# Layer norm of x in a Mamba scan kernel: two steps on VectorE, the power on GpSimd, taken earlier

## The chip, the cores and the metric

The kernel runs on one core of a Trainium2 chip. The metric is the device time of one execution in microseconds (us). Engines are named as the profile names them: PE is TensorE's matmul (PEld its weight load), DVE is VectorE, ACT is ScalarE, POOL is GpSimd, SP is SyncE, which issues the loads and stores here.

## The reference

One transformer-like block over x of 2 x 4096 x 256 in fp32. Only the first line bears on the change:

```python
h = _layernorm(x, axis=-1) * (1 + ca) + sa        # (x - m) / sqrt(v + 1e-5) over the 256 features
x = x + ga * _L0_attn_ref(h, ...)                 # two Mamba scans (backward and forward), sigmoid, mean, norm
h = _layernorm(x, axis=-1) * (1 + cb) + sb
x = x + gb * _L0_ffn_ref(h, ...)                  # 256 -> 1024 gated -> 1024 -> 1024 -> 256
```

Each Mamba scan projects h to 512 inner channels, convolves over time, and runs the recurrence `h = a * h + bx` for 16 states of each channel.

## The kernel before

Time is cut into chunks of 512 steps. There are 8 chunks for each of two batches, so 16 in a pass. Pass one (`ps == 0`) runs the backward scan, and pass two the forward scan. After both, a second stage does the join and the feed-forward layers, also in 16 chunks.

In a pass, the work of one chunk is written out by hand as 32 units (`NU`), numbered k = 0 to 31. A unit is one of 16 states for one half of the channels. It has two scan tiles of 128 x 512, one after the other on DVE (steps 2k and 2k+1). Every engine has its own loop over the units and runs it in order; semaphores tie the loops together:

- POOL, at unit k: `weigh_b(k)` makes the product dBx that the scan of unit k adds (for 27 of 32 units, `B_UNITS`; the other five, 19, 22, 25, 28 and 31, take it from PE). Then `weigh_c(k - 4)` scales the scanned state of 12 of the units (`P_UNITS`: 1, 2, 5, 9, 13, 15, ...). Then, at some units, small steps for the next chunks.
- ACT, at step g = 2k or 2k+1: `decay(g)` makes the exponentials that scan tile g needs, at most three tiles ahead of DVE (it waits until tile g - 3 is scanned). Behind it come the evacuations of the next chunk's matmuls.
- DVE, at unit k: the two scans (`scan`), which wait for the product (`dbx`) and for the decays (`da`); gates of some units; `weigh_c(k - 4)` for the other 20 units; at last the norm's step of this unit.
- PE does the projections, the convolution and the transposes of the states.

The norm of x runs two chunks ahead, only in pass one: in 14 of its chunks, for the chunk two further on. The first two chunks' norms are done in the prologue. The steps, all counted on the one semaphore `ln`, are:

1. DVE at unit 4: four `bn_stats` (L1435). At unit 5: four `bn_aggr` (L1441), which leave the mean in `mv[:, :, 0]` and the variance in `mv[:, :, 1]`. DVE does these at the end of the unit, behind its scans.
2. POOL at unit 8 (`RSTD_S`), behind `weigh_b(8)` and `weigh_c(4)` (unit 4 is not one of POOL's, so only `weigh_b(8)` stands there): four operations on 128 x 4 values, L1317 adds epsilon, L1319 raises to the power -1/2, L1321 multiplies by the mean, L1323 multiplies by -1.
3. ACT at step 18 (`AT_XN`), that is unit 9, behind `decay(18)` and other work of that step: `norm_x` waits for `ln` to reach 6 and writes the normalised x in four activations (L1165). The next item in ACT's order is `decay(19)`.
4. SP stores it (`store_xn`), and PE transposes it one chunk later (`front`).

Of the kernel before, what the change touches and what calls it, by code (L numbers as in the profile page):

```python
# [9 lines left out]
ALU = mybir.AluOpType  # L10
# [2 lines left out]
P = 128  # L13
BATCH, SEQ, DM = 2, 4096, 256
DI, DS, DCONV, DTR, DH = 512, 16, 4, 64, 1024
LNK = 7
T = 512
NC = SEQ // T
NCH = BATCH * NC
# [9 lines left out]
EPS = 1e-5  # L29
# [44 lines left out]
AT_XN = 18  # L74
AT_EXP = (51, 57)
AT_LNP = (51, 57)
NORM_STAT, NORM_AGGR, RSTD_S = 4, 5, 8
AT_XD = (15, 19, 20, 21)
ADD_S = (29, 0)
U_S = (30, 11)  # L80
# [284 lines left out]
def mamba(nc, a, bank, ident, cols, mod, gain, norm_c, fcol, any_odd, passes, w1, w2, J, x_v, yb_v, yf_v, xn_v, b_dram,  # L365
# [11 lines left out]
    with ExitStack() as c:  # L377
        def sb(name, shape):
            return c.enter_context(nc.sbuf_tensor(f"m_{name}", shape, F32))
# [7 lines left out]
        mv = sb("mv", [P, TS, 6])  # L387
# [161 lines left out]
        def _(sp):  # L549
# [8 lines left out]
            def load_x(ch):  # L558
                if rev(ch):
                    wait(sp, S["ln"], ch.at(LNK, 0))  # L560
                    sp.dma_start(xy[:, :, :], x_v[ch.batch, ch.time(True)]).then_inc(S["x_in"], 16)
# [8 lines left out]

            def store_xn(ch):

                sp.wait_ge(S["ln"], ch.at(LNK, 7))
                sp.dma_start(xn_v[ch.batch, ch.time(True)], xn[:, :, :]).then_inc(S["xn_out"], 16)

            def store_b(ch):
# [178 lines left out]
        def _(pe):  # L755
# [15 lines left out]
            def front(ch, g):  # L771
                q = ch.batch
                for k in range(KM):
                    if g == AT_LN[k]:

                        if k == 0:
                            if rev(ch):
                                pe.wait_ge(S["ln"], ch.at(LNK, 7))
                            else:
                                pe.wait_ge(S["xn_in"], ch.local(16, 16))  # L780
                        turn(J_LN[k], lambda s: xn[:, s, k * P:(k + 1) * P], ch)
                for m in range(KI):
                    k = g - AT_X[m]
                    if 0 <= k < KM:
                        if m == 0:
                            if ch.opens() and ch.batch == 0 and k == 0:
                                pe.wait_ge(S["w_in"], 48 * (ch.ps + 1))
                            wait_drained(pe, ch, J_LN[k])
                        part(ch, J_X[m], k, KM, w_in[:, k, m * P:(m + 1) * P], hT[:, k, :])
                    k = g - AT_CONV[m]  # L790
                    if 0 <= k < DCONV:

                        if k == 0:
                            if m == 0:
                                if ch.opens() and ch.batch == 0:
                                    pe.wait_ge(S["init"], SINIT + ch.ps)
                                pe.wait_ge(S["halo"], ch.at(2, 1))
                            if BANK[J_X[m]] != BANK[J_CONV[m]]:

                                wait_drained(pe, ch, J_X[m])  # L800
                        o = HALO - k if rev(ch) else k
                        part(ch, J_CONV[m], k, DCONV, diag[:, m * DCONV + k, :], xpre[:, m, o:o + T])
                    if g == (FIRST_DT if ch.first() else AT_DT)[m]:
                        if m == 0:
                            wait_drained(pe, ch, J_B)
                        part(ch, J_DT[m], 0, 1, w_dt[:, m * P:(m + 1) * P], dbB[0:DTR, :])
                    k = g - (FIRST_Z if ch.first() else AT_Z)[m]
                    if 0 <= k < KM:
                        part(ch, J_Z[m], k, KM, w_in[:, k, (KI + m) * P:(KI + m + 1) * P], hT[:, k, :])
                    if g == AT_B + m:  # L810

                        pe.wait_ge(S["xi"], ch.at(2, m // 2 + 1))
                        part(ch, J_B, m, KI, w_x[:, m, :], xi[:, m, :], B0 + 2 * DS)
                if g == (FIRST_C if ch.first() else AT_C):
                    rows = B0 + 2 * DS
                    wait_drained(pe, ch, J_B)
                    wait_free(pe, ch, J_C)
                    for t in range(TS):
                        mm = pe.transpose(FB[BANK[J_C]][:, t * rows:(t + 1) * rows], dbB[0:rows, t * P:(t + 1) * P],
                                          ident[0:rows, 0:rows])  # L820
                    mm.then_inc(fill[BANK[J_C]], 1)
# [188 lines left out]
        def _(act):  # L1010
# [145 lines left out]
            def norm_x(ch):  # L1156

                wait(act, S["xn_out"], ch.at(16, 0))
                if not ch.first():
                    act.sem_inc(S["go"], 1)  # L1160
                    wait_filled(act, ch.go(-1), J_LN[1])
                    act.sem_inc(S["go"], 1)
                act.wait_ge(S["ln"], ch.at(LNK, 6))
                for s in range(TS):
                    ins = act.activation(xn[:, s, :], xy[:, s, :], ACT.Identity, scale=mv[:, s, 3:4], bias=mv[:, s, 5:6])  # L1165
                ins.then_inc(S["ln"], 1)
# [146 lines left out]
        def _(pool):  # L1313
            def norm(ch):

                pool.wait_ge(S["ln"], ch.at(LNK, 2))
                pool.tensor_tensor(mv[:, :, 2], mv[:, :, 1], norm_c[:, 0, :], ALU.add).then_inc(S["ln"], 1)  # L1317
                pool.wait_ge(S["ln"], ch.at(LNK, 3))
                pool.tensor_tensor(mv[:, :, 3], mv[:, :, 2], norm_c[:, 1, :], ALU.pow).then_inc(S["ln"], 1)  # L1319
                pool.wait_ge(S["ln"], ch.at(LNK, 4))  # L1320
                pool.tensor_tensor(mv[:, :, 4], mv[:, :, 0], mv[:, :, 3], ALU.mult).then_inc(S["ln"], 1)  # L1321
                pool.wait_ge(S["ln"], ch.at(LNK, 5))
                pool.tensor_tensor(mv[:, :, 5], mv[:, :, 4], norm_c[:, 2, :], ALU.mult).then_inc(S["ln"], 1)  # L1323

            def add_dt(ch, half):
                q = ch.batch
# [102 lines left out]
        def _(dve):  # L1429
            def norm(ch, slot):  # L1430
                if slot == NORM_STAT:
                    dve.wait_ge(S["x_in"], ch.at(16, 16))
                    wait(dve, S["ln"], ch.at(LNK, 0))
                    for s in range(TS):
                        ins = dve.bn_stats(stat[:, s, :], xy[:, s, :])  # L1435
                    ins.then_inc(S["ln"], 1)
                if slot == NORM_AGGR:
                    dve.wait_ge(S["ln"], ch.at(LNK, 1))
                    dve.sem_inc(S["go"], 1)
                    for s in range(TS):  # L1440
                        ins = dve.bn_aggr(mv[:, s, 0:2], stat[:, s, :])  # L1441
                    ins.then_inc(S["ln"], 1)

            def gate(ch, g, m):
                q = ch.batch
                if g == AT_Y[m] + DVE_LAG:
                    dve.wait_ge(S["z"], ch.at(2, m // 2 + 1))
                    wait_filled(dve, ch, J_Y[m])
                    dve.tensor_tensor(z[:, q, m, :], FB[BANK[J_Y[m]]][:, :], z[:, q, m, :], ALU.mult
                                      ).then_inc(drain[BANK[J_Y[m]]], 1)  # L1450
# [31 lines left out]
            def body(ch):  # L1482
                for k in range(NU):
                    for m in range(2):
                        g = 2 * k + m
                        scan(ch, k, m)
                        if has(ch, -1):
                            for i in (2, 3):
                                gate(ch.go(-1), g, i)
                        for i in range(2):  # L1490
                            gate(ch, g, i)
                    old = unit(ch, k - W_LAG)
                    if old:
                        weigh_c(*old)
                    if norms(ch, 2):
                        norm(ch.go(2), k)

            def find_odd(n):

# [11 lines left out]
            def prologue(ch):  # L1511
# [2 lines left out]
                dve.memset(one_r[:, :], 1.0).then_inc(S["odd"], 1)  # L1514
                for s in range(NU):
                    norm(ch, s)
                dve.wait_ge(S["cols_in"], 32)
                for k in range(KI * DCONV):
                    ins = dve.tensor_scalar(diag[:, k, :], ident[:, :], cols[:, 0, COL_CW + k:COL_CW + k + 1], None, ALU.mult)
# [5 lines left out]
                for n in range(NPIECE):  # L1525
                    find_odd(n)
                    if n == 2:
                        for k in range(KM):
                            for b in range(BATCH):
                                last = dve.tensor_scalar(cbc[:, k, b, :], ident[:, :], 0.0, cs[:, k, b:b + 1], ALU.mult, ALU.add)  # L1530
                        last.then_inc(S["bcast_c"], 1)
                    if n == 3:
                        for s in range(NU):
                            norm(ch.go(1), s)
                dve.wait_ge(S["p_sum"], 2 * NPIECE)
                dve.tensor_reduce(odd_sum[:, :], YB[1][0:1, :], mybir.AxisListType.X, ALU.add).then_inc(S["odd"], 1)
                dve.wait_ge(S["odd"], 2)
# [371 lines left out]
```

## Time and profile before

| | |
|---|---|
| median of 3 runs | 4685.21 us (4684.75 to 4686.28) |
| the profiled execution | 4683.44 us |
| its span, first to last instruction | 4681.6 us |
| mean granted TensorE clock | 0.988 |
| PE, DVE, ACT, POOL busy, share of the span | 95%, 81%, 70%, 71% |

The two passes take the span up to about 3356 us, the feed-forward stage the rest. Shares of the whole span mix the two: POOL is almost unused in the second stage, PE almost never idle there. The stage that matters for the change is pass one, from about 76 to 1508 us, and there one chunk lasts 103.3 us.

### The profile page before, as it was taken

The page shows a single profiled execution, that of the slowest core. Times are in us where ns is not written, and L with a number is a line of the kernel's source. Part 1 is how long each engine was busy: PE and PEld are TensorE (multiplying, and loading weights), DVE is VectorE, ACT ScalarE, POOL GpSimd, SP SyncE. Part 2 cuts the span into 40 slices and gives each one's busy share as a digit, 9 for nine tenths or more (in the row PEclk, how much of TensorE's full clock was granted, in tenths as well). Part 3 has the DMA queues.
Part 4 walks back from the last instruction along what each step waited for, and adds up shares of the span by engine and source line. Part 5 has one row for each costly group of instructions (what it writes and reads, how often), then busy time and mean ns, then how long its engine had stood idle before and what let it go on. Part 6 is the DMA issues. An engine that isn't in the chain of part 4 may idle for free. (4 is left out here: it accounts for less than half of the span.)

```text
span 4681.6 us, 69073 instructions
## 1 busy us (share of the span) xinstructions
PE 4451.6 (95%) x24932; PEld 3375.9 (72%) x24932; DVE 3800.5 (81%) x4136; ACT 3279.4 (70%) x7067; POOL 3321.1 (71%) x1599
## 2 busy tenths in 40 slices
PE   8999999999999999999999999998899999999999
PEld 3676666667666666776666676666688888888888
DVE  6999999999999999999999999999754545444442
ACT  6788888888888877888888888888544444444443
POOL 5999999999999999999999999999710000000000
PEclk9999999999999999999999999999999999999999
DMA  8545444444554444444444445445411101010100
GB/s 296 175 136 150 146 142 138 141 136 140 148 146 138 147 138 140 136 143 143 138 139 132 135 137 147 142 134 158 164 62 35 34 23 37 32 37 32 37 23 10
DMA packets 297752, 545.90 MB, mean 117 GB/s; under 512 B 101888, under 2 KB 186624, under 8 KB 262784
## 3 DMA queue, kind: packets, MB, share of 16 engines
q1 hardware_dynamic: 296512, 529.91, 37.3%
q10 hardware_dynamic: 896, 11.54, 0.7%
q8 instruction: 199, 3.26, 0.3%
q14 instruction: 145, 1.19, 0.1%
HBM read 502.77 MB, written 50.14 MB: 118 GB/s over the span
## 5 line engine op out<-in xcount | busy, mean ns | idle before, releaser
L1472 DVE TENSOR_TENSOR_SCAN m_h<-bank,m_dBx 128x512 f32<-128x512 f32 x1728 | 2004.3, 1203 | 112.3 <-ACT bank L1205 82.4
L904 PEld LDWEIGHTS bank<-ident,m_h 128*128 128x128 f32 x8192 | 972.1, 142 | 514.5 <-issue 370.5
L904 PE MATMUL bank<-ident,m_h 128*128 128x128 f32 x8192 | 1203.6, 276 | 63.8 <-DVE m_h L1480 50.4
L1363 POOL TENSOR_TENSOR m_dBx<-u,m_Bs 128x1024 f32<-128x1024 f32 x432 | 1019.2, 2385 | 1.1 <-DVE m_h L1472 0.9
L1363 POOL TENSOR_TENSOR m_dBx<-m_u,m_Bs 128x1024 f32<-128x1024 f32 x432 | 1018.5, 2384 | 0.0
L1374 POOL TENSOR_TENSOR m_h<-m_h,m_Cs 128x1024 f32<-128x1024 f32 x384 | 912.7, 2377 | 37.9 <-ACT m_state L1119 37.4
L1480 DVE TENSOR_TENSOR m_h<-m_h,bank 128x1024 f32<-128x1024 f32 x640 | 768.9, 1201 | 22.8 <-PE bank L886 16.9
L311 POOL TENSOR_TENSOR mvj<-mvj,norm_c 128x4 f32<-128x4 f32 x16 | 16.6, 1035 | 970.9 <-DVE mvj L272 970.9
L1205 ACT ACTIVATE bank<-dt,cols 128x511 f32<-128x511 f32 (+1 forms) x864 | 593.5, 689 | 19.0 <-DVE m_h L1472 18.3
L1205 ACT ACTIVATE bank<-m_dt,cols 128x511 f32<-128x511 f32 (+1 forms) x864 | 593.6, 689 | 18.7 <-DVE m_h L1472 18.1
L886 PEld LDWEIGHTS bank<-ident,m_Ct 128*128 128x128 f32 x2560 | 303.5, 138 | 336.1 <-issue 212.7
L767 PE MATMUL bank<-hT,w_in 128*128 128x512 f32 x1024 | 533.4, 621 | 5.2 <-ACT hT L1034 2.9
L767 PE MATMUL bank<-xpre,diag 128*128 128x512 f32 x1024 | 518.4, 595 | 0.0
L886 PE MATMUL bank<-ident,m_Ct 128*128 128x128 f32 x2560 | 393.6, 277 | 84.8 <-DVE m_h L1480 83.4
L1666 PE MATMUL bank<-gb,h 128*128 128x512 f32 x2048 | 468.3, 390 | 0.0
L1666 PE MATMUL bank<-ga,h 128*128 128x512 f32 x2048 | 467.6, 389 | 0.0
L1666 PEld LDWEIGHTS bank<-ga,h 128*128 128x128 f32 x2048 | 384.4, 188 | 80.4
L1666 PEld LDWEIGHTS bank<-gb,h 128*128 128x128 f32 x2048 | 383.4, 188 | 78.8
L1812 DVE TENSOR_TENSOR ga<-raw,ga 128x512 fp32r<-128x512 f32 x256 | 177.5, 693 | 302.6 <-ACT raw L1749 301.1
L1202 ACT COPY bank<-m_edge 128x1 f32<-128x1 f32 x1512 | 240.3, 159 | 234.5 <-DVE m_h L1472 234.5
L851 PE MATMUL bank<-m_dg,m_uT 128*128 128x128 f32 x2560 | 343.9, 277 | 38.6 <-DVE m_h L1472 38.6
L1472 DVE TENSOR_TENSOR_SCAN m_h<-m_h,bank 128x512 f32<-128x512 f32 x320 | 371.2, 1199 | 0.7 <-PE bank L851 0.6
(189 smaller groups left out, 5933.7 us busy)
## 6 DMA issues: line engine op xcount, KB each, us to landing
m_Bs<-b_dram SPq DMA_DIRECT2D x256, 1024.0 KB, 5.4
m_Cs<-c_dram SPq DMA_DIRECT2D x384, 256.0 KB, 3.5
m_dg<-d_dram SPq DMA_DIRECT2D x160, 256.0 KB, 3.7
xx<-in_x SPq DMA_DIRECT2D x16, 512.0 KB, 5.4
xn_dram<-xx SPq DMA_DIRECT2D x16, 512.0 KB, 3.3
yb_dram<-m_ysb SPq DMA_DIRECT2D x16, 512.0 KB, 3.3
xx<-xn_dram SPq DMA_DIRECT2D x16, 512.0 KB, 3.8
x_dram<-m_ysb SPq DMA_DIRECT2D x16, 512.0 KB, 3.3
```

What stands on the lines that cost most here:

```text
L767: mm = pe.matmul(FB[BANK[i]][0:rows, :], lhsT, rhs, start=(k == 0), stop=(k == kn - 1))
L851: mm = pe.matmul(DA[tile % NDA][:, s * P:(s + 1) * P], uT[:, s, m * P:(m + 1) * P], dg[:, n % NDG, s, :], start=True, stop=True)
L886: mm = pe.matmul(CB[:, t * P:(t + 1) * P], Ct[:, ch.batch, t, s:s + 1].broadcast_to((P, P)), ident[:, :], start=True, stop=True, is_transp ...
L904: mm = pe.matmul(YB[b][:, o:o + P], h[:, k % NH, m, tok:tok + P], ident[:, :], start=(s == 0 and o == 0), stop=False, is_transpose=True, s ...
L1202: act.copy(out[:, t:t + 1], edge[:, j, m:m + 1])
L1205: act.activation(out, src, ACT.Exp, scale=cols[:, ch.ps, col:col + 1]).then_inc(S["da"], 1)
L1363: pool.tensor_tensor(dBx[:, dbx_ring(ch, k) % NDBX, :, :], u[ch.batch][:, m, :], Bs[:, k // BP % 2, k % BP, :].unsqueeze(1).broadcast_to(( ...
L1374: pool.tensor_tensor(o, o, Cs[:, i % 2, :].unsqueeze(1).broadcast_to((P, 2, T)), ALU.mult).then_inc(S["weigh_p"], 1)
L1472: dve.tensor_tensor_scan(o, decays, share, initial, ALU.mult, ALU.add).then_inc(S["scan"], 1)
L1480: dve.tensor_tensor(o, o, CB[:, :].unsqueeze(1).broadcast_to((P, 2, T)), ALU.mult).then_inc(S["weigh_d"], 1)
L1666: return pe.matmul(out, lhsT, rhs, start=start, stop=stop)
L1812: dve.tensor_tensor(dst[:, 1], raw[:, j % XR, :], dst[:, 0].bitcast(F32), ALU.subtract).then_inc(S["lo"], 1)
```

## The change

The norm of x is divided anew between DVE and POOL. DVE adds epsilon behind unit 6 (`NORM_EPS`), POOL only takes the power, at unit 6 in place of unit 8 (`RSTD_S`), and DVE multiplies mean, -1 and power in one operation behind unit 8 (`NORM_BIAS`). The semaphore `ln` now counts 6 steps a chunk in place of 7; ACT's `norm_x` waits for the fifth, which is DVE's last step.

```diff
-LNK = 7
+LNK = 6
-NORM_STAT, NORM_AGGR, RSTD_S = 4, 5, 8
+NORM_STAT, NORM_AGGR, NORM_EPS, RSTD_S, NORM_BIAS = 4, 5, 6, 6, 8
...
 def norm_x(ch):
...
-                act.wait_ge(S["ln"], ch.at(LNK, 6))
+                act.wait_ge(S["ln"], ch.at(LNK, 5))
...
             def norm(ch):
-                pool.wait_ge(S["ln"], ch.at(LNK, 2))
-                pool.tensor_tensor(mv[:, :, 2], mv[:, :, 1], norm_c[:, 0, :], ALU.add).then_inc(S["ln"], 1)
                 pool.wait_ge(S["ln"], ch.at(LNK, 3))
                 pool.tensor_tensor(mv[:, :, 3], mv[:, :, 2], norm_c[:, 1, :], ALU.pow).then_inc(S["ln"], 1)
-                pool.wait_ge(S["ln"], ch.at(LNK, 4))
-                pool.tensor_tensor(mv[:, :, 4], mv[:, :, 0], mv[:, :, 3], ALU.mult).then_inc(S["ln"], 1)
-                pool.wait_ge(S["ln"], ch.at(LNK, 5))
-                pool.tensor_tensor(mv[:, :, 5], mv[:, :, 4], norm_c[:, 2, :], ALU.mult).then_inc(S["ln"], 1)
...
+            def norm_rest(ch, slot):
+                if slot == NORM_EPS:
+                    dve.wait_ge(S["ln"], ch.at(LNK, 2))
+                    dve.tensor_scalar(mv[:, :, 2], mv[:, :, 1], EPS, 1.0, ALU.add, ALU.mult).then_inc(S["ln"], 1)
+                if slot == NORM_BIAS:
+                    dve.wait_ge(S["ln"], ch.at(LNK, 4))
+                    dve.scalar_tensor_tensor(out=mv[:, :, 5], in0=mv[:, :, 0], scalar=-1.0, in1=mv[:, :, 3],
+                                             op0=ALU.mult, op1=ALU.mult).then_inc(S["ln"], 1)
```

`norm_rest(ch, k)` is called right behind DVE's `norm(ch, k)`, in the units of a chunk and at both places of the prologue. `store_xn` on SP and `front` on PE wait for the full count, now 6.

## Rows read from the trace of the kernel before

**Rows 1.** The page: busy time of each engine over the whole span.
```profile
PE 4451.6 (95%) x24932; PEld 3375.9 (72%) x24932; DVE 3800.5 (81%) x4136; ACT 3279.4 (70%) x7067; POOL 3321.1 (71%) x1599
```

**Rows 2.** Windows, a chunk of each pass: PE, PEld, DVE, ACT, POOL busy, clock, DMA.
```profile
888.55:991.81 103.26, 96.13 (x582) 69.83 (x581) 98.75 (x97) 86.00 (x204) 102.03 (x51) 1.00 0.50 142
...
2627.72:2729.41 101.69, 97.26 (x583) 71.03 (x581) 97.67 (x89) 83.84 (x200) 100.34 (x46) 0.98 0.46 137
```

**Rows 3.** Timeline of POOL in the chunk of pass one: start, duration, instruction.
```profile
911.78 2.38 POOL L1374 TENSOR_TENSOR m_h<-m_h,m_Cs 128x1024 f32<-128x1024 f32 x1
914.10 4.72 POOL L1363 TENSOR_TENSOR m_dBx<-u,m_Bs 128x1024 f32<-128x1024 f32 x2
918.75 0.23 POOL L1317 TENSOR_TENSOR m_mv<-m_mv,norm_c 128x4 f32<-128x4 f32 x1
919.06 1.02 POOL L1319 TENSOR_TENSOR m_mv<-m_mv,norm_c 128x4 f32<-128x4 f32 x1
920.16 0.20 POOL L1321 TENSOR_TENSOR m_mv<-m_mv 128x4 f32<-128x4 f32 x1
920.44 0.20 POOL L1323 TENSOR_TENSOR m_mv<-m_mv,norm_c 128x4 f32<-128x4 f32 x1
920.59 2.37 POOL L1363 TENSOR_TENSOR m_dBx<-u,m_Bs 128x1024 f32<-128x1024 f32 x1
...
932.19 4.73 POOL L1363 TENSOR_TENSOR m_dBx<-u,m_Bs 128x1024 f32<-128x1024 f32 x2
...
959.06 2.38 POOL L1374 TENSOR_TENSOR m_h<-m_h,m_Cs 128x1024 f32<-128x1024 f32 x1 [0.99 <-ACT m_state L1119]
```

**Rows 4.** Timeline of DVE in the same chunk: units 6 and 7, 8's weighing, 9, 12, 16, 26.
```profile
915.64 4.52 DVE L1472 TENSOR_TENSOR_SCAN m_h<-bank,m_dBx 128x512 f32<-128x512 f32 x4
...
924.04 1.19 DVE L1480 TENSOR_TENSOR m_h<-m_h,bank 128x1024 f32<-128x1024 f32 x1
925.16 2.32 DVE L1472 TENSOR_TENSOR_SCAN m_h<-bank,m_dBx 128x512 f32<-128x512 f32 x2
...
936.94 2.34 DVE L1472 TENSOR_TENSOR_SCAN m_h<-bank,m_dBx 128x512 f32<-128x512 f32 x2 [2.16 <-POOL m_dBx L1363]
...
950.41 2.34 DVE L1472 TENSOR_TENSOR_SCAN m_h<-bank,m_dBx 128x512 f32<-128x512 f32 x2 [1.05 <-ACT bank L1205]
...
979.94 1.22 DVE L1472 TENSOR_TENSOR_SCAN m_h<-bank,m_dBx 128x512 f32<-128x512 f32 x1 [0.28 <-ACT bank L1205]
981.70 3.45 DVE L1472 TENSOR_TENSOR_SCAN m_h<-bank,m_dBx 128x512 f32<-128x512 f32 x3 [0.54 <-ACT bank L1205]
```

**Rows 5.** Timeline of ACT in the same chunk, from step 18 to step 24.
```profile
920.29 0.69 ACT L1205 ACTIVATE bank<-dt,cols 128x511 f32<-128x511 f32 x1
922.29 0.69 ACT L1057 ACTIVATE m_u<-bank,cols 128x512 f32<-128x512 f32 x1 [1.31 <-PE bank L767]
922.88 0.18 ACT L1119 COPY m_state<-m_h 128x4 f32<-128x4 f32 x1
922.96 2.08 ACT L1165 ACTIVATE xx<-xx,m_mv 128x256 f32<-128x256 f32 x4
...
925.02 0.68 ACT L1205 ACTIVATE bank<-dt,cols 128x511 f32<-128x511 f32 x1
...
936.11 0.69 ACT L1205 ACTIVATE bank<-dt,cols 128x511 f32<-128x511 f32 x1
```

**Rows 6.** Instructions on tile mvj (feed-forward stage): duration ns min/median/max.
```profile
L276 DVE SCALAR_TENSOR_TENSOR x<-x,mvj,gain x64: 475/477/485, 3361.3 to 4542.8; 128x256 f32<-128x256 f32 x64
...
L272 DVE TENSOR_SCALAR mvj<-mvj x16: 170/171/172, 3360.0 to 4540.0; 128x4 f32<-128x4 f32 x16
```

**Rows 7.** Timeline of DVE in the prologue: checks of the weights, behind idle time.
```profile
17.25 4.87 DVE L1509 TENSOR_TENSOR m_h<-m_h,m_dBx 128x1024 bf16<-128x1024 f32 x4 [5.69 <-ACT m_dBx L1280]
...
39.98 2.36 DVE L1509 TENSOR_TENSOR m_Bs<-m_Bs,m_dBx 128x1024 bf16<-128x1024 f32 x2 [6.33 <-ACT m_dBx L1280]
```

**Rows 8.** Tile m_mv: count of DVE's statistics over the run.
```profile
L1441 DVE BATCH_NORM_AGGREGATE m_mv<-m_stat x64: 139/146/182, 7.6 to 1432.1; 128x2 f32<-128x6 f32 x64
```

More of the change, by code:

```diff
@@ L571, in store_xn @@
             def store_xn(ch):
-                sp.wait_ge(S["ln"], ch.at(LNK, 7))
+                sp.wait_ge(S["ln"], ch.at(LNK, LNK))
                 sp.dma_start(xn_v[ch.batch, ch.time(True)], xn[:, :, :]).then_inc(S["xn_out"], 16)
@@ L777, in front @@
                             if rev(ch):
-                                pe.wait_ge(S["ln"], ch.at(LNK, 7))
+                                pe.wait_ge(S["ln"], ch.at(LNK, LNK))
                             else:
@@ L1496, in body @@
                         norm(ch.go(2), k)
+                        norm_rest(ch.go(2), k)
             def find_odd(n):
@@ L1516, in prologue @@
                     norm(ch, s)
+                    norm_rest(ch, s)
                 dve.wait_ge(S["cols_in"], 32)
@@ L1534, in prologue @@
                             norm(ch.go(1), s)
+                            norm_rest(ch.go(1), s)
                 dve.wait_ge(S["p_sum"], 2 * NPIECE)
```

## The prediction, made before the changed kernel was run

> **What bounds the kernel now.** I read the page first, then the windows of one chunk, then the timelines of POOL, DVE and ACT in that chunk. The shares of the whole span [rows 1] mislead, since they average the scan stage with the feed-forward stage. In a chunk of pass one POOL is busy 102.03 of 103.26 us, DVE 98.75, PE 96.13 and ACT 86.00 [rows 2]. POOL looks like the bound. The reader should see in the timelines that it is not the one that sets the pace where the norm stands.
>
> Take the waits in order. DVE scans units 6 and 7 without a gap; the scans start every 1.11 us, so unit 7 starts at 915.64 + 2 x 1.11 = 917.86 [rows 4]. The product of unit 7 was started by POOL at 914.10 and lasts 2.36 (half of 4.72), so it was ready at 916.46, 1.4 us ahead of need [rows 3, 4]. DVE then stands idle once, 2.16 us before the scan of unit 12 at 936.94 [rows 4]. The view puts this down to POOL, but unit 12's product is the first of the two that start at 932.19, so it was ready at 934.55 [rows 3]. What came last is ACT's decay of step 24, 936.11 + 0.69 = 936.80, and the scan starts 0.14 later [rows 4, 5]. From `norm_x` at 922.96 to that decay ACT works without a gap that the view shows (I quote its ends; in the full answer 21 rows lie between these two, and none has an idle note) [rows 5]. So at unit 12 DVE waits for ACT, and ACT's chain begins with `norm_x`. POOL in turn stands idle 0.99 us before 959.06, for a state that ACT copies behind DVE's scans [rows 3]: POOL runs ahead of DVE and is stopped by it. The pace in this stretch is ACT, then DVE. POOL has about 1 us to spare in a chunk.
>
> **The change part by part.**
>
> *POOL gives up three operations.* Before, the norm holds POOL from 918.75 to 920.59, which is 1.84 us [rows 3]. The power alone is 1.02 us, about 0.97 from start to start, since independent records overlap by 0.05 (920.44 + 0.20 against 920.59) [rows 3]. It saves 0.87 us a chunk. On an engine that is stopped for 0.99 us once a chunk anyway [rows 3], this alone is worth nothing, unless POOL were the bound: then 14 x 0.87 = 12 us.
>
> *The power moves from behind unit 8's product to ahead of unit 7's.* POOL reaches that place when `weigh_c(2)` of 911.78 is over, at 914.10 [rows 3]. But it now needs epsilon's sum, which DVE makes behind its second scan of unit 6, at 917.86 at the earliest [rows 4]. The same form of operation, a tensor_scalar on 128 x 4, takes 171 ns [rows 6], so the sum is there at 918.03. A dependent step follows 0.08 later (920.08 to 920.16 [rows 3]). The power runs from 918.11 to 919.13. POOL has stood idle 4.0 us, and queued behind it are the products of units 7, 8 and all later ones. Unit 7's product starts at about 919.1, in place of 914.10, and is ready at 921.45.
>
> *DVE stalls.* The scan of unit 7 waits for that product: it starts at about 921.5 in place of 917.86, 3.65 us late. This includes the 0.12 us that the new small step costs from start to start. Unit 8's product is ready 2.33 later, at 923.8, ahead of its scan, which is 3.65 late too.
>
> *ACT stalls, with more behind it.* `norm_x` now waits for the bias, which DVE makes behind the weighing of unit 8. Before, this weighing starts at 924.04, and the place behind it is 925.16 [rows 4]. Before, `norm_x` ran at 922.96, so it stood 2.2 us ahead of that place [rows 5]. Now the place is at 925.16 + 3.65 = 928.81. The bias is a scalar_tensor_tensor on 128 x 4 that no row shows. It is bounded by the 146 ns of the aggregate on two values [rows 8] and by the 477 ns of the same operation on 256 [rows 6]; I take 0.17, as it is nearest in size to the tensor_scalar of 171 [rows 6]. So the bias is there at 928.98, and ACT starts at 929.06, 6.1 us later than 922.96. With the bounds it is 6.08 to 6.4. Everything that ACT had in line behind it, decay 19 first, is 6.1 late. DVE's scan of step 19 was at 926.27 (925.16 + 1.11) and now finds its decay only at 925.70 + 6.1 = 931.8, so DVE stalls some 1.8 us more. ACT's line has no slack up to step 24, so the scan of unit 12 starts at 936.94 + 6.1 = 943.0.
>
> *What absorbs it?* DVE's 2.16 us of idle time at unit 12 is idle for ACT, and moves with it. The waits after it, 1.05 at unit 16 and 0.54 with 0.28 before it at unit 26, are for ACT too [rows 4], and ACT follows DVE there. POOL, only 3.1 us late by then (4.0 less 0.87), is stopped before 959.06 for 0.99 + 3.0 us, and is then as late as DVE. The next chunk starts with all engines 6.1 later in the same order. If the 0.82 us at unit 26 were all regained, 5.3 us would remain.
>
> *The two added steps on DVE,* 0.12 to 0.17 us each, are inside these numbers. The Trainium skill, page "DVE: VectorE Perf Modes", section "The TRN2 errata", gives 58 + N cycles at 0.96 GHz, an estimate of 65 ns for four values, where the row shows 171 [rows 6]; by it the two steps together would take 0.2 us a chunk less, 3 us in all.
>
> *The prologue* does two norms. DVE waits there for POOL's power, some 1.5 us each time with the bias. The first is covered by 5.69 us of idle time and the second by 6.33 [rows 7]: nothing. Without that cover it would be 3 us. SP's `store_xn` comes 6.1 later, in front of loads of products that POOL needs only at unit 16, itself 3 late or more: nothing. Pass two and the feed-forward stage keep their work.
>
> **The sum.** DVE's aggregates number 64 [rows 8], four a norm: 16 norms, two in the prologue, 14 in chunks. 14 x 6.1 = 85 us. Against the profiled execution 4683.44 + 85 = 4768.4; that execution is 1.8 below the median of 4685.21, against which I state the forecast: **4770 us**, 1.8% slower. The chunk would last 109.4 us in place of 103.3. With 5.3 a chunk it is 4759, with 6.4 it is 4775. A change under 0.2% (9 us) can't be told from none.
>
> **The rivals.**
>
> *Only the first stall counts.* The product of unit 7 is late but ACT's wait for the bias is somehow hidden. ACT would then be driven by DVE's tiles alone: decay 18 waits for tile 15, 3.65 late, and with the conv copy behind it `norm_x` would start at about 925.2, 2.3 late. 14 x 2.3 = 32 us: 4717. For it speaks that ACT has 1.31 us of idle time at 922.29 [rows 5], against it that the bias can't be there before unit 8's weighing is done. Chance 0.09, with all cases between 4695 and 4750.
>
> *POOL is the bound after all (faster).* It is one mechanism: POOL reaches unit 6 no earlier than DVE leaves it, the power never waits, and 0.87 us a chunk come back: 4673. It would decide if DVE's second scan of unit 6 ended before POOL came free at 914.10; the rows have it at 917.9 [rows 3, 4], 3.8 later. POOL's 102.03 of 103.26 us speak for it [rows 2]. The Trainium skill, "Perfetto Trace Analysis", section "Identifying the Most-Contended Engine", says to improve the engine with the highest occupancy first, which is POOL here; the stop of 0.99 us before 959.06 speaks against taking it so. Chance 0.04.
>
> *The stalls are swallowed (no change).* DVE's 2.16 us and POOL's 0.99 us would take them if the lateness at unit 12 were under 2.16. The first stall alone brings 3.65. Chance 0.04.
>
> *Worse than the sum.* A wait that I count as covered joins the line: PE's convolution behind ACT's late copies, or a load behind `store_xn`; one more us a chunk is 14 us: 4784. Chance 0.09, for all above 4777.
>
> *The forecast:* 4750 to 4777, chance 0.74.
>
> **How the numbers follow.** The forecast and the near ends of its neighbours must hold 8 in 10: I take 4735 to 4782. Faster 0.04, within 0.2% 0.04, slower 0.92.
>
> **What would show it.** In the profile after: POOL idle about 4.0 us before the power, released by DVE; DVE idle about 3.5 us before the scan of unit 7, released by POOL's product, and about 1.8 us before the second scan of unit 9, released by ACT; ACT idle 3 to 4 us before `norm_x`, released by DVE; a chunk of pass one of 109.4 us and one of pass two of 101.7 as before [rows 2]. I would be wrong if `norm_x` were not the head of ACT's line to step 24, which the chunk's length would tell: 105.6 with the first stall alone, 102.4 if POOL were the bound.

## The result, and the profile after

The changed kernel takes 4789.2 us (median of 4 runs, 4788.4 to 4789.3), against 4685.0 before (4 runs). The ratio is 1.0223, 95% interval 1.021 to 1.0235. It is slower, as forecast, but by 104 us where 85 were forecast, and it lies above the range (4735 to 4782). The span of the profiled execution is 4787.4 us.

The windows of two chunks of pass one (length, then busy time of PE, PEld, DVE, ACT and POOL, granted clock, DMA share and rate), to be held against [rows 2]:

```profile
944.60:1055.67 111.07, 100.14 (x578) 72.15 (x577) 100.79 (x99) 85.60 (x203) 100.98 (x46) 0.95 0.46 131
1389.41:1500.48 111.07, 98.33 (x582) 70.69 (x581) 100.98 (x99) 86.09 (x204) 101.55 (x47) 0.98 0.47 133
```

The chunk lasts 111.07 us in place of 103.26: 7.8 more, where 6.1 were forecast. POOL's busy time fell by 1.05 us (0.5 in the second row), and the chunk grew all the same. DVE's grew by 2.04 us for two operations on four values a partition, and that is far too much for them. The granted clock reads 0.95 in the first row and 1.00 in the chunk shown of before, and PE's matmuls on 128 x 512 (L767) last longer, 660 and 630 ns at the mean in place of 597 and 593. The length of the chunk doesn't follow the clock: it is 111.07 at 0.95 and at 0.98. A chunk of pass two lasts 101.7 as before.

POOL's timeline in the first of the two chunks. L1317 is now the power, L1357 makes the products, L1368 weighs states:

```profile
974.20 1.02 POOL L1317 TENSOR_TENSOR m_mv<-m_mv,norm_c 128x4 f32<-128x4 f32 x1 [3.98 <-DVE m_mv L1441]
975.19 6.99 POOL L1357 TENSOR_TENSOR m_dBx<-u,m_Bs 128x1024 f32<-128x1024 f32 x3
...
984.44 4.69 POOL L1357 TENSOR_TENSOR m_dBx<-u,m_Bs 128x1024 f32<-128x1024 f32 x2
...
1017.67 2.37 POOL L1368 TENSOR_TENSOR m_h<-m_h,m_Cs 128x1024 f32<-128x1024 f32 x1 [4.02 <-ACT m_state L1119]
```

The power waited 3.98 us for epsilon; the forecast was 4.0. The last row answers to the one at 959.06 of [rows 3]: POOL's stop there grew from 0.99 to 4.02 us. With this one, POOL's stops in the chunk now add up to 10.0 us (3.98, 0.89, 4.02 and 1.10), in place of 0.99.

DVE's timeline. L1441 is epsilon, L1444 the bias, L1475 the scans:

```profile
971.74 2.31 DVE L1475 TENSOR_TENSOR_SCAN m_h<-bank,m_dBx 128x512 f32<-128x512 f32 x2
973.97 0.15 DVE L1441 TENSOR_SCALAR m_mv<-m_mv 128x4 f32<-128x4 f32 x1
977.63 2.34 DVE L1475 TENSOR_TENSOR_SCAN m_h<-bank,m_dBx 128x512 f32<-128x512 f32 x2 [3.51 <-PE bank L904]
...
983.84 1.20 DVE L1483 TENSOR_TENSOR m_h<-m_h,bank 128x1024 f32<-128x1024 f32 x1
984.95 1.89 DVE L1444 SCALAR_TENSOR_TENSOR m_mv<-m_mv 128x4 f32<-128x4 f32 x1
986.76 1.21 DVE L1475 TENSOR_TENSOR_SCAN m_h<-bank,m_dBx 128x512 f32<-128x512 f32 x1
989.65 1.22 DVE L1475 TENSOR_TENSOR_SCAN m_h<-bank,m_dBx 128x512 f32<-128x512 f32 x1 [1.68 <-ACT bank L1205]
...
1000.84 2.34 DVE L1475 TENSOR_TENSOR_SCAN m_h<-bank,m_dBx 128x512 f32<-128x512 f32 x2 [0.51 <-PE bank L904]
```

The reader is to see three things. The scan of unit 7 stalls 3.51 us (forecast 3.5). The view names PE, but the product that POOL started at 975.19 was ready at about 977.55, 0.08 before the scan. The second scan of unit 9 stalls 1.68 (forecast 1.8). And between them the bias lasts 1.89 us, where 0.17 were forecast: it ends at 986.84, and POOL's first product of the pair from 984.44 ends at about 986.8.

ACT's timeline, against [rows 5]:

```profile
981.29 0.18 ACT L1119 COPY m_state<-m_h 128x4 f32<-128x4 f32 x1
986.88 2.07 ACT L1165 ACTIVATE xx<-xx,m_mv 128x256 f32<-128x256 f32 x4 [5.40 <-DVE m_mv L1444]
...
988.94 0.68 ACT L1205 ACTIVATE bank<-dt,cols 128x511 f32<-128x511 f32 x1
...
1000.01 0.69 ACT L1205 ACTIVATE bank<-dt,cols 128x511 f32<-128x511 f32 x1
```

`norm_x` waits 5.40 us for the bias; the forecast was 3 to 4. On the clock of the chunk it starts at 986.88 - 944.60 = 42.28, before at 922.96 - 888.55 = 34.41: 7.87 late. The line behind it is again free of idle time up to the decay of step 24 (1000.01 + 0.69 = 1000.70), and unit 12's scan starts 0.14 later, at 56.24 on the chunk's clock against 48.39: 7.85 late. That is the chunk's growth.

The instructions on tile m_mv, with minimum, median and maximum in ns:

```profile
L1441 DVE TENSOR_SCALAR m_mv<-m_mv x16: 151/164/172, 8.1 to 1529.8; 128x4 f32<-128x4 f32 x16
L1317 POOL TENSOR_TENSOR m_mv<-m_mv,norm_c x16: 1014/1020/1025, 8.3 to 1530.1; 128x4 f32<-128x4 f32 x16
L1444 DVE SCALAR_TENSOR_TENSOR m_mv<-m_mv x16: 168/1866/1889, 9.4 to 1540.8; 128x4 f32<-128x4 f32 x16
```

The bias takes 168 ns in the prologue, where POOL stands still, and 1866 at the median. Epsilon takes 164: it runs while POOL waits for it.

### The profile page after: what moved, and what is told of

Same layout as the page of the kernel before. It is cut to its first block and busy times, and to the rows that moved or that the text cites. A ratio compares the mean times of both kernels' runs of the same rounds, so it can differ in the third digit from the quotient of the medians.

```text
span 4787.4 us, 69057 instructions
## 1 busy us (share of the span) xinstructions
PE 4486.0 (94%) x24932; PEld 3391.6 (71%) x24932; DVE 3832.1 (80%) x4168; ACT 3280.2 (69%) x7067; POOL 3311.6 (69%) x1551
## 5 line engine op out<-in xcount | busy, mean ns | idle before, releaser
L1475 DVE TENSOR_TENSOR_SCAN m_h<-bank,m_dBx 128x512 f32<-128x512 f32 x1728 | 2012.8, 1210 | 182.9 <-ACT bank L1205 124.9
L904 PEld LDWEIGHTS bank<-ident,m_h 128*128 128x128 f32 x8192 | 979.2, 143 | 528.2 <-issue 380.9
L904 PE MATMUL bank<-ident,m_h 128*128 128x128 f32 x8192 | 1210.5, 277 | 70.6 <-DVE m_h L1483 57.1
L1357 POOL TENSOR_TENSOR m_dBx<-u,m_Bs 128x1024 f32<-128x1024 f32 x432 | 1016.8, 2374 | 6.6 <-DVE m_h L1475 6.0
L1357 POOL TENSOR_TENSOR m_dBx<-m_u,m_Bs 128x1024 f32<-128x1024 f32 x432 | 1016.8, 2377 | 6.5 <-DVE m_h L1475 6.2
L1368 POOL TENSOR_TENSOR m_h<-m_h,m_Cs 128x1024 f32<-128x1024 f32 x384 | 910.1, 2370 | 87.3 <-ACT m_state L1119 86.6
L767 PE MATMUL bank<-xpre,diag 128*128 128x512 f32 x1024 | 541.7, 617 | 28.3 <-DVE m_z L1452 28.1
L767 PE MATMUL bank<-hT,w_in 128*128 128x512 f32 x1024 | 529.0, 616 | 4.7 <-ACT hT L1034 3.2
L1475 DVE TENSOR_TENSOR_SCAN m_h<-m_h,bank 128x512 f32<-128x512 f32 x320 | 372.1, 1206 | 0.7 <-PE bank L851 0.7
```

Source lines behind the costliest of these rows:

```text
L767: mm = pe.matmul(FB[BANK[i]][0:rows, :], lhsT, rhs, start=(k == 0), stop=(k == kn - 1))
L904: mm = pe.matmul(YB[b][:, o:o + P], h[:, k % NH, m, tok:tok + P], ident[:, :], start=(s == 0 and o == 0), stop=False, is_transpose=True, s ...
L1357: pool.tensor_tensor(dBx[:, dbx_ring(ch, k) % NDBX, :, :], u[ch.batch][:, m, :], Bs[:, k // BP % 2, k % BP, :].unsqueeze(1).broadcast_to(( ...
L1368: pool.tensor_tensor(o, o, Cs[:, i % 2, :].unsqueeze(1).broadcast_to((P, 2, T)), ALU.mult).then_inc(S["weigh_p"], 1)
L1475: dve.tensor_tensor_scan(o, decays, share, initial, ALU.mult, ALU.add).then_inc(S["scan"], 1)
```

## The experiments

The two questions were whether the two waits in a line (POOL's for epsilon, ACT's for the bias) carry the loss as the forecast had it, and why the bias is eleven times as long as it should be. An operation is called held below where it lasts far longer than the same operation does beside an idle POOL, and DVE does nothing else meanwhile. Chunk lengths below are those of a chunk in the middle of pass one, from first scan to first scan in the timeline. Each time stands against the kernel before on the same chip, 4684.6 to 4685.5 us.

**A probe of small operations on DVE.** The kernel before, with operations on a scratch tile that nobody reads:

```diff
+                if k == 8:
+                    dve.scalar_tensor_tensor(out=probe[:, :, 2], in0=probe[:, :, 0], scalar=-1.0, in1=probe[:, :, 1],
+                                             op0=ALU.mult, op1=ALU.mult)
+                if k == 9:
+                    dve.tensor_scalar(probe[:, :, 3], probe[:, :, 0], EPS, 1.0, ALU.add, ALU.mult)
+                if k == 10:
+                    for s in range(TS):
+                        dve.tensor_scalar(probe[:, s, 4:5], probe[:, s, 0:1], probe[:, s, 1:2], -1.0, ALU.mult, ALU.mult)
+                if k == 14:
+                    dve.scalar_tensor_tensor(out=probe[:, :, 5], in0=probe[:, :, 0], scalar=-1.0, in1=probe[:, :, 1],
+                                             op0=ALU.mult, op1=ALU.mult)
+                if k == 20:
+                    dve.tensor_tensor(probe[:, :, 6], probe[:, :, 0], probe[:, :, 1], ALU.mult)
```

> The kernel before, with small operations on 128 x 4 values of a scratch tile added on DVE, which nobody waits for: behind unit 8 a scalar_tensor_tensor with two inputs in SBUF, behind unit 9 a tensor_scalar with constants, behind unit 10 four tensor_scalar with pointer scalars, behind unit 14 the scalar_tensor_tensor again, behind unit 20 a plain two-input multiply. Two-input theory (the changed kernel's bias lasted 1.87 us because a DVE operation with two SBUF inputs is held while a POOL operation runs, and goes on only when that ends): the two-input ones take from 0.2 to 2.3 us, by where they fall in POOL's operation, and each ends within 0.1 us of the end of a POOL operation; the one-input ones take 0.15 to 0.17 us at any place. Rival (the place or the form as such costs 1.87): the scalar_tensor_tensor takes 1.87 at both places, without regard to POOL, or only behind unit 8. If DVE's idle time before unit 12 covers the added work, the time is within 5 us of before's; if not, up to 14 x 2 = 28 us more.

Tile probe of this kernel, in the order of units 10, 8, 9, 14 and 20:

```profile
L1508 DVE TENSOR_SCALAR probe<-probe x56: 194/198/203, 107.0 to 1527.5; 128x1 f32<-128x1 f32 x56
L1502 DVE SCALAR_TENSOR_TENSOR probe<-probe x14: 159/2132/2166, 99.3 to 1519.1; 128x4 f32<-128x4 f32 x14
L1505 DVE TENSOR_SCALAR probe<-probe x14: 165/1874/1894, 103.6 to 1522.0; 128x4 f32<-128x4 f32 x14
L1510 DVE SCALAR_TENSOR_TENSOR probe<-probe x14: 2380/4718/6778, 120.2 to 1540.2; 128x4 f32<-128x4 f32 x14
L1513 DVE TENSOR_TENSOR probe<-probe x14: 1215/1309/1691, 146.9 to 1559.3; 128x4 f32<-128x4 f32 x14
```

The timelines of DVE and of POOL in one chunk (this one lasts 112.5 us, most of the others 108.9):

```profile
973.10 2.13 DVE L1502 SCALAR_TENSOR_TENSOR probe<-probe 128x4 f32<-128x4 f32 x1
...
977.99 1.87 DVE L1505 TENSOR_SCALAR probe<-probe 128x4 f32<-128x4 f32 x1
...
996.25 4.72 DVE L1510 SCALAR_TENSOR_TENSOR probe<-probe 128x4 f32<-128x4 f32 x1
```

```profile
972.85 4.67 POOL L1364 TENSOR_TENSOR m_dBx<-u,m_Bs 128x1024 f32<-128x1024 f32 x2
977.48 2.35 POOL L1346 TENSOR_TENSOR u<-dt,m_xi 128x1024 f32<-128x1024 f32 x1
...
996.28 2.35 POOL L1375 TENSOR_TENSOR m_h<-m_h,m_Cs 128x1024 f32<-128x1024 f32 x1
998.60 2.35 POOL L1364 TENSOR_TENSOR m_dBx<-u,m_Bs 128x1024 f32<-128x1024 f32 x1
```

The scalar_tensor_tensor ends at 975.23, and POOL's first product of the pair at about 975.2. The tensor_scalar with constants ends at 979.86, and POOL's 977.48 + 2.35 at 979.83. The one of unit 14 ends at 1000.97, and POOL's 998.60 + 2.35 at 1000.95: it stayed held through a whole further POOL operation. So these operations do last until a POOL operation beside them ends, and not always the first one. My two-input theory was too narrow: the tensor_scalar has one tensor input and is held as well. Only the one with a single value a partition is free, at 0.20 us. The rival of a fixed 1.87 us falls, since the same operation takes 0.16 to 6.8.

The time was 4762.2 us, a single run; the forecast had 28 us more than before at most, and it was 77. DVE spends 10.0 us a chunk in the four held operations by their medians, not the 2 or so that I counted, since I took a hold to end with POOL's current operation.

**The power back at POOL's unit 8.**

```diff
-NORM_STAT, NORM_AGGR, NORM_EPS, RSTD_S, NORM_BIAS = 4, 5, 6, 6, 8
+NORM_STAT, NORM_AGGR, NORM_EPS, RSTD_S, NORM_BIAS = 4, 5, 6, 8, 8
```

> The changed kernel with the power back at POOL's unit 8, so that it no longer waits for epsilon. My theory (two waits in a line: the power behind DVE's unit 6, then norm_x at the head of ACT's line behind the bias): the first wait is gone (3.65 us), and the second stays, with the bias from 925.3 on the clock of before's chunk, held to POOL's next end at about 926.8, and norm_x 3.9 us late: a chunk of about 107.2 us, 55 us over before, about 4740. Rival (the power's early wait is the whole loss, the bias wait is covered once it is gone): a chunk of 103.3 to 104, 4683 to 4695.

It took 4739.8 us, ratio 1.0116 (1.0099 to 1.0133), and 107.3 us a chunk. The first wait is gone, and the second stays: `norm_x` is 4.0 us late. DVE's timeline:

```profile
949.87 0.94 DVE L1441 TENSOR_SCALAR m_mv<-m_mv 128x4 f32<-128x4 f32 x1
...
958.05 0.87 DVE L1444 SCALAR_TENSOR_TENSOR m_mv<-m_mv 128x4 f32<-128x4 f32 x1
958.84 1.21 DVE L1475 TENSOR_TENSOR_SCAN m_h<-bank,m_dBx 128x512 f32<-128x512 f32 x1
961.73 1.22 DVE L1475 TENSOR_TENSOR_SCAN m_h<-bank,m_dBx 128x512 f32<-128x512 f32 x1 [1.68 <-ACT bank L1205]
```

Epsilon now runs beside a busy POOL and is held for 0.94 us in place of 0.15. This is the same operation at the same place: only POOL's state differs. The bias in turn is held for 0.87 us in place of 1.87, since it falls later into POOL's product. So of the 3.8 us a chunk by which this run is shorter than the changed kernel, 1.0 comes from the bias's hold and 2.8 from the first wait, less epsilon's hold.

**The bias by POOL, right behind the early power.**

```diff
                 pool.tensor_tensor(mv[:, :, 3], mv[:, :, 2], norm_c[:, 1, :], ALU.pow).then_inc(S["ln"], 1)
+                pool.wait_ge(S["ln"], ch.at(LNK, 4))
+                pool.tensor_tensor(mv[:, :, 4], mv[:, :, 0], mv[:, :, 3], ALU.mult).then_inc(S["ln"], 1)
+                pool.wait_ge(S["ln"], ch.at(LNK, 5))
+                pool.tensor_tensor(mv[:, :, 5], mv[:, :, 4], norm_c[:, 2, :], ALU.mult).then_inc(S["ln"], 1)
...
-                if slot == NORM_BIAS:
...
```

> The changed kernel, but with the bias again by POOL's two operations right behind the early power; epsilon stays with DVE behind unit 6. My theory: the first wait stays (power from 14.1 to 18.1 on the chunk's clock) and unit 7's product is some 4.2 us late, but norm_x no longer waits for DVE's unit 8 and comes about 2.8 us late, set by the decays behind unit 7's scans: a chunk of about 106.1 us, 4720 to 4726. Rival (only POOL's order counts, ACT's line does not): the bias's place changes nothing, and the chunk is near 111 us as in the changed kernel, or longer by POOL's 0.6 us: 4789 to 4797.

It took 4742.7 us, ratio 1.0123 (1.0106 to 1.014), some 20 us above what I expected; the chunks last 108.1 and 107.0 by turns. The first step came out: `norm_x` starts at 37.32 on the chunk's clock, 2.9 late. What I missed is behind it. DVE's timeline in front of unit 12:

```profile
970.12 1.22 DVE L1483 TENSOR_TENSOR m_h<-m_h,bank 128x1024 f32<-128x1024 f32 x1 [1.58 <-PE bank L886]
...
975.71 2.34 DVE L1475 TENSOR_TENSOR_SCAN m_h<-bank,m_dBx 128x512 f32<-128x512 f32 x2 [1.01 <-ACT bank L1205]
```

DVE waits 1.58 us for PE's spread of c, and 0.48 in the next chunk. ACT, behind `norm_x`, waits for PE's convolution, 1.85 us in this chunk and 0.76 in the next:

```profile
968.75 0.69 ACT L1057 ACTIVATE m_u<-bank,cols 128x512 f32<-128x512 f32 x1 [1.85 <-PE bank L767]
...
1075.71 0.69 ACT L1057 ACTIVATE u<-bank,cols 128x512 f32<-128x512 f32 x1 [0.76 <-PE bank L767]
```

These two waits are what the expected 106.1 us lacks, to within 0.2 us. PE is late because DVE's stall at unit 7 leaves it idle for 3.29 us before 959.56 (3.30 before 1067.62), and it comes back at a lower clock. The windows of the 6 us behind this idle time, in the two chunks:

```profile
959.56:965.56 6.00, 6.00 (x20) 4.37 (x21) 6.00 (x6) 6.00 (x17) 6.00 (x4) 0.52 0.41 143
1067.62:1073.62 6.00, 6.00 (x25) 4.05 (x26) 6.00 (x6) 6.00 (x17) 6.00 (x4) 0.72 0.44 116
```

The granted clock reads 0.52 in one and 0.72 in the other, so PE ran nearly all of the first stretch at the lower of its two levels, 1.2 GHz, and little more than half of the second. Four matmuls of L904 that start 3.6 us into it take 1.06 us in the first and 0.60 in the second. The rival (111 us a chunk whatever the bias's place) falls. Why the clock comes back sooner in every other chunk no run shows.

**The bias as four one-value operations, in its place.**

```diff
-                    dve.scalar_tensor_tensor(out=mv[:, :, 5], in0=mv[:, :, 0], scalar=-1.0, in1=mv[:, :, 3],
-                                             op0=ALU.mult, op1=ALU.mult).then_inc(S["ln"], 1)
+                    for s in range(TS):
+                        ins = dve.tensor_scalar(mv[:, s, 5:6], mv[:, s, 0:1], mv[:, s, 3:4], -1.0, ALU.mult, ALU.mult)
+                    ins.then_inc(S["ln"], 1)
```

> The changed kernel with the bias as four tensor_scalar operations of one SBUF tensor input and a pointer scalar each, in the same place. Two-input theory: the four together take 0.3 to 0.5 us in place of 1.87, norm_x comes 1.4 us earlier, the chunk lasts about 109.6 us, and the time is about 4769. Rival (the place costs it, whatever the form): they take 1.87 us or more together and the time stays at 4789 or above.

It took 4772.2 us, ratio 1.0185 (1.0168 to 1.0202), and 109.8 us a chunk. DVE's timeline has all four in 0.57 us:

```profile
977.84 0.57 DVE L1445 TENSOR_SCALAR m_mv<-m_mv 128x1 f32<-128x1 f32 x4
```

The four run inside one of POOL's products, 0.53 us behind its start, as the bias of the changed kernel does, and are not held; they take a little more than the 0.3 to 0.5 us that I expected. So the hold is worth 17 us of the 104, against this form, and 14 x (1.87 - 0.17) = 24 us against the 0.17 us of the forecast.

**Everything earlier.** Epsilon behind unit 5, the power at unit 7, the bias behind unit 7; first with the changed kernel's operations, then with both of DVE's steps in the one-value form.

```diff
-NORM_STAT, NORM_AGGR, NORM_EPS, RSTD_S, NORM_BIAS = 4, 5, 6, 6, 8
+NORM_STAT, NORM_AGGR, NORM_EPS, RSTD_S, NORM_BIAS = 4, 5, 5, 7, 7
```

> The changed kernel with the same operations at other units: epsilon on DVE behind unit 5, right behind the aggregates; the power on POOL at unit 7; the bias on DVE behind unit 7. On the clock of before's chunk POOL comes to the power at 16.4 + 900 and epsilon is there at about the same time, so the power does not wait, and the bias is asked for 1.2 us before norm_x's place. My theory (order and two waits in a line are the loss, and the held operations only add to them): a chunk of 103.3 us if both held operations (epsilon up to 0.7 us, bias up to 0.9) fit in DVE's 2.16 us of idle time before unit 12, up to 104.8 if the bias misses the gap between two POOL operations: 4682 to 4707. Rival (two small steps on DVE beside a busy POOL cost their holds on the path wherever they stand): at least 1.6 us a chunk, 4707 or more.

> As the one before, with epsilon and bias as four operations of one value a partition each, which were not held beside POOL in the probe (0.20 us each, 0.12 from start to start). My theory: nothing is held, DVE has 1.0 us more in its idle time, the chunk lasts 103.3 us as before the change, and the time is within 5 us of 4685. POOL's saved 0.87 us brings nothing, since POOL is stopped behind DVE anyway. Rival (POOL is the bound once the waits are gone): 102.4 us a chunk, 4673.

They took 4686.4 us (ratio 1.0001, 0.9991 to 1.0011) and 4684.6 us (0.9997, 0.9987 to 1.0006), with 103.4 and 103.3 us a chunk. The whole loss is gone with the division of work left as the change made it. DVE's timeline of the first, and then of the second:

```profile
917.01 0.77 DVE L1441 TENSOR_SCALAR m_mv<-m_mv 128x4 f32<-128x4 f32 x1
...
923.27 0.29 DVE L1444 SCALAR_TENSOR_TENSOR m_mv<-m_mv 128x4 f32<-128x4 f32 x1
```

```profile
922.74 0.57 DVE L1447 TENSOR_SCALAR m_mv<-m_mv 128x1 f32<-128x1 f32 x4
...
938.09 2.34 DVE L1478 TENSOR_TENSOR_SCAN m_h<-bank,m_dBx 128x512 f32<-128x512 f32 x2 [1.27 <-ACT bank L1205]
```

The idle time before unit 12 has shrunk from 2.16 [rows 4] to 1.27 us, which is where DVE's added work went. POOL's work fell by 0.87 us, and its stops in the later half grew from 0.99 [rows 3] to 0.73 + 1.10: what it saves, it waits.

**`norm_x` later.** ACT's `norm_x` at step 45 in place of 18, with SP's store moved to just ahead of `store_y`; in the kernel before, then in the early one-value form.

```diff
-AT_XN = 18
+AT_XN = 45
...
-                if norms(ch, 2):
-                    store_xn(ch.go(2))
...
                 load_c(ch, 9)
+                if norms(ch, 2):
+                    store_xn(ch.go(2))
                 if has(ch, -1):
                     store_y(ch.go(-1))
```

> The kernel before, with ACT's norm_x at step 45 in place of 18, and SP's store of it ahead of the store of y. My theory (norm_x heads ACT's line to the decay of step 24, for which DVE stands idle 2.16 us): without norm_x in that line a chunk of pass one comes near one of pass two, less what DVE's statistics (1.6 us) and POOL's norm (1.84 us) add: 102.2 to 102.6 us, 10 to 15 us less in all, 4670 to 4675. Rival (POOL set the pace of pass one, as the view's note at unit 12 says): nothing changes, 103.3 us and 4685.

> The early one-input form together with the late norm_x. If, with norm_x out of ACT's line, DVE and ACT bind: DVE carries 1.0 us more than in the kernel before with late norm_x, and the chunk lasts 102.2 to 103.2 us, 4670 to 4684, not below the run with late norm_x alone. If POOL binds once the line is shorter, its saved 0.87 us shows at last: 101.7 us a chunk, 4663.

They took 4679.3 us (ratio 0.9986, 0.9976 to 0.9995) and 4676.5 us (0.998, 0.9971 to 0.999), with 102.8 us a chunk each, so a gain of 6 and of 9 us. For the first the direction is as expected and the size about half: I had taken a chunk of pass two as the floor. The second lies in its range, but 2.8 us below the first and not above it, with intervals that overlap. The scan of unit 12 still waits for ACT in both, here in the first and then in the second:

```profile
931.68 2.34 DVE L1472 TENSOR_TENSOR_SCAN m_h<-bank,m_dBx 128x512 f32<-128x512 f32 x2 [1.64 <-ACT bank L1205]
```

```profile
931.89 2.34 DVE L1478 TENSOR_TENSOR_SCAN m_h<-bank,m_dBx 128x512 f32<-128x512 f32 x2 [0.73 <-ACT bank L1205]
```

So with 2.08 us of `norm_x` out of its line, ACT came only 0.5 us earlier: another wait of ACT had taken its place. In the first run it is one for POOL. ACT's timeline and POOL's:

```profile
927.49 1.06 ACT L1102 ACTIVATE m_xi<-m_u 128x1024 f32<-128x1024 f32 x1 [0.91 <-POOL u L1345]
```

```profile
925.10 2.36 POOL L1345 TENSOR_TENSOR u<-dt,m_xi 128x1024 f32<-128x1024 f32 x1
```

From there ACT works without idle time up to the decay of step 24. So once `norm_x` has left the line, POOL does set unit 12's start in the first run, by way of ACT. In the second POOL comes to this step earlier, and ACT waits there no more; but DVE carries 0.9 us more, ACT waits 0.41 us for DVE's tiles in its place, and the chunk is shorter by only 0.05. This pair of runs changed both loads at once, so it doesn't tell how far POOL alone would go.

**The changed kernel with the late `norm_x`.** The edit is the same, on the changed kernel.

> The changed kernel with norm_x at step 45 in place of 18 (and its store ahead of the store of y); epsilon, power and bias stay where the change put them. My theory (two waits in a line): the power still waits 4.0 us for epsilon and unit 7's scan is still 3.5 us late, the bias is still held for 1.87, but nothing in ACT's line waits for the bias any more. DVE comes to unit 9 5.5 us late and has 2.16 us of idle time before unit 12; ACT's decays follow DVE's tiles: a chunk of 106.7 to 107.4 us in place of 111.07, 4732 to 4742. Rival (POOL's late products alone carry the loss, ACT's line does not count): the chunk stays at 111 us and the time at 4789.

It took 4740.7 us, ratio 1.0116 (1.0099 to 1.0133), with 107.4 us in most chunks. The DVE timeline shows both early troubles unchanged, and the wait at unit 9 gone:

```profile
955.03 2.34 DVE L1475 TENSOR_TENSOR_SCAN m_h<-bank,m_dBx 128x512 f32<-128x512 f32 x2 [3.52 <-PE bank L904]
...
962.36 1.88 DVE L1444 SCALAR_TENSOR_TENSOR m_mv<-m_mv 128x4 f32<-128x4 f32 x1
964.16 2.32 DVE L1475 TENSOR_TENSOR_SCAN m_h<-bank,m_dBx 128x512 f32<-128x512 f32 x2
```

Moving `norm_x`, and with it the wait for the bias, out of ACT's line gives back 48 of the 104 us. The same move gave 6 us in the kernel before and 8 in the early one-value form, so some 40 of the 48 are the wait's. With POOL's late products as the only cause it would have given no more than those 6 to 8.

## Why the prediction was right in kind and wrong in size

*What bounds the kernel* held. POOL was busiest and not the bound: the two early forms took 0.87 us off it a chunk and gained nothing that can be measured, while DVE's added work went into its wait for ACT at unit 12. The view's note at unit 12 pointed to POOL, and the ACT decay was the cause. The run with late `norm_x` shows it: unit 12's wait became shorter. But POOL is close behind: in that run ACT's line is stopped for 0.91 us by POOL.

*The power's wait* was 3.98 us (4.0), *DVE's stall at unit 7* 3.51 (3.5), *the stall at unit 9* 1.68 (1.8). Putting the power back at unit 8 takes the first two away and gives 49 us back, of which about 14 (14 x 1.0) are the bias's shorter hold. The rival with the first stall alone was priced too low, at 2.3 us a chunk: with the bias by POOL, and `norm_x` 2.9 late, the chunk grew by 3.7 and 4.8 by turns, since ACT then waits for PE.

*ACT's line behind `norm_x`* held: its lateness went to unit 12 without loss (7.87 and 7.85 us), and nothing of it was regained later in the chunk.

*The step that failed* is the size of one term, "the bias is a scalar_tensor_tensor on 128 x 4 that no row shows", taken at 0.17 us with a bound of 0.48. It measured 1.87, since DVE is held there until the running POOL operation ends. 6.1 + 1.7 is 7.8 us a chunk, which is what was measured. 14 x 7.8 would be 109 us; the first chunk grew by 4.8 only (102.7 in place of 97.9), the second by 7.2, the one behind the last norm by 1.6, and the prologue was 2.7 shorter, with the first scan at 73.03 us in place of 75.76. The latter can't be put down to the change: two runs with the norm of before, the probe and the one with late `norm_x`, had it at 73.88 and 73.75, and the other runs with the changed prologue between 74.3 and 76.4.

The value of 0.17 and the upper bound were wrong because their rows were made while POOL stood still: L272 and L276 [rows 6] come from the feed-forward stage, where POOL is almost unused. The lower bound, the aggregate's 146 ns [rows 8], was made beside a busy POOL; it has one input in SBUF and was not held. The trace of before did hold a hint that I passed over: in the prologue, POOL's small operations beside DVE's two-input checks of the weights took up to 1052 ns in place of 204. DVE's timeline and POOL's there:

```profile
31.30 2.36 DVE L1509 TENSOR_TENSOR m_Bs<-m_Bs,m_dBx 128x1024 bf16<-128x1024 f32 x2 [0.86 <-ACT m_dBx L1280]
```

```profile
31.89 0.69 POOL L1321 TENSOR_TENSOR m_mv<-m_mv 128x4 f32<-128x4 f32 x1
32.66 1.05 POOL L1323 TENSOR_TENSOR m_mv<-m_mv,norm_c 128x4 f32<-128x4 f32 x1
```

The Trainium skill, "SBUF — State Buffer", section "Who interferes with whom", says that a DVE operation with two SBUF inputs contends with a GpSimd operation that reads SBUF, that one in a mode that uses two ports contends with GpSimd too, and that the one that issues later is blocked until the other is through. By that rule the bias would have been about 1.9 us in the forecast, and the sum 109 us, an estimate: behind the power, three products and a weighing of 2.33 us each take POOL to 928.4, and the product that starts there, in which the bias of 928.81 falls, runs to 930.7. The traces agree that operations with two SBUF inputs are held; that tensor_scalar is held on 128 x 4 and not on 128 x 1 they show too, but no run shows which mode either was in. That the hold can pass over one or two further POOL operations (4.7 and 6.8 us) goes beyond the rule.

The page of the Trainium skill that the prediction calls "DVE: VectorE Perf Modes" has the title "VectorE: DVE Perf Modes". Its formula gave 65 ns for four values; epsilon measured 164 (median), and the measurement decides.

*What stays open:* why the hold sometimes goes past the end of POOL's current operation, and why PE's clock comes back sooner in every other chunk of the run with the bias by POOL.

## What to carry to other kernels

A small step that moves between engines brings a wait with it, and the wait's price is set by the loops it ties together: put the producer's step early enough that the consumer never asks first, and look at what else stands in the consumer's queue. On VectorE, take the price of a small operation only from rows in which GpSimd was busy in the same way. The busiest engine need not be the bound if it is stopped once a round; before relieving it, look for the stop, and for how much another engine still waits for it.

## What the runs showed of the hardware that I had not expected

- A DVE operation on four values a partition lasted 0.29 to 4.7 us at the median beside a POOL that works without a break, by how far POOL's operation had come, and 0.14 to 0.17 beside an idle one. Held were scalar_tensor_tensor and tensor_tensor with two SBUF inputs, and tensor_scalar with constants on 128 x 4 (1.87 us, and 0.94 and 0.77 at other places). Not held was tensor_scalar on 128 x 1 (0.20 us). Every hold ended within 0.04 us of the end of a POOL operation.
- An operation that began on DVE 0.06 us before one POOL operation ended and 0.03 us before the next began (996.25 against 996.28) was held for 4.72 us, to the end of the second POOL operation behind it; the longest hold, of 6.78 us, overlapped three.
